# Value products on two column halves of TensorE, normalised from PSUM by VectorE

## The reference, cut to what matters

```python
y = x * rsqrt(mean(x * x, -1) + 1e-6) * rms_w            # x: 2 x 1024 x 512, float32
q, k, v = split(einsum('bsm,cm->bsc', y, w_in))          # 32 query heads in 8 groups, 8 k/v heads, 64 wide
q, k = rope(q), rope(k)                                  # per group: 4 query heads share one k and one v
qk = where(causal, q @ k^T * 64 ** -0.5, -inf)           # 1024 x 1024 per head
attn = softmax(qk)
o = einsum('bghsp,bgxpd->bghsd', attn, v)                # the value products
x = layernorm(x + (x + einsum('bsc,mc->bsm', o, w_out)))
x = layernorm(x + ternary(x) @ (ternary(weight) + rram_variation)^T)
```

## Time and profile before

| | us |
|---|---|
| median of 3 runs | 1427.19 (1426.4 to 1428.69) |
| span of the profiled execution, first to last instruction | 1425.4 |
| first value product starts at | 58.1 |
| TensorE, VectorE, ScalarE, GpSimd busy | 1318.0, 1147.2, 1116.3, 873.7 |
| TensorE's granted clock, mean of the span | 0.982 |

### The profile page before, as it was taken

The page is one execution under the profiler, slowest core; times in us unless marked ns, Lnnn a source line. Parts: engine busy times, 40 slices in busy tenths (PEclk is TensorE's granted clock), DMA queues, the critical chain, the costliest instruction groups (busy, mean ns, idle before and its releaser), DMA issues. The chain is left out here.

```text
span 1425.4 us, 25329 instructions
## 1 busy us (share of the span) xinstructions
PE 1318.0 (92%) x7328; PEld 838.4 (59%) x7328; DVE 1147.2 (80%) x3062; ACT 1116.3 (78%) x2327; POOL 873.7 (61%) x905
## 2 busy tenths in 40 slices
PE   4689999999999999999999999999999999898886
PEld 2456565665656565665656565666656566565554
DVE  4578887878887888878887888878788787887976
ACT  4768878788888888788887878788887888787664
POOL 1266667386645766386646766387646767786565
PEclk9799999999999999999999999999999999999998
DMA  6101111011101211021101211021100211210002
GB/s 199 27 20 38 64 30 31 27 57 45 37 21 45 59 29 31 23 60 44 36 24 26 72 35 31 23 60 43 38 24 23 75 35 37 61 42 27 18 33 85
DMA packets 45163, 61.82 MB, mean 43 GB/s; under 512 B 10464, under 2 KB 27104, under 8 KB 45024
## 3 DMA queue, kind: packets, MB, share of 16 engines
q1 hardware_dynamic: 45024, 60.20, 14.3%
HBM read 34.74 MB, written 4.46 MB: 27 GB/s over the span
## 5 line engine op out<-in xcount | busy, mean ns | idle before, releaser
L1100 DVE SCALAR_TENSOR_TENSOR prob_lo<-t,prob_hi 128x512 f16<-128x512 f32 x576 | 394.7, 686 | 76.0 <-ACT prob_hi L797 72.2
L797 ACT ACTIVATE prob_hi<-t 128x512 f16<-128x512 f32 x576 | 340.2, 591 | 146.1 <-PE t L1221 140.8
L1165 PE MATMUL s<-k_t,q_t 128*128 128x512 f32 (+3 forms) x1536 | 428.2, 383 | 23.8 <-DVE neg_max L1009 8.5
L829 ACT ACTIVATE prob<-prob,neg_max 128x896 f32<-128x896 f32 (+7 forms) x512 | 392.0, 767 | 7.2 <-DVE neg_max L1009 4.3
L1221 PE MATMUL t<-ident,prob 128*128 128x128 f32 x2304 | 350.8, 275 | 6.9 <-ACT prob L829 6.8
L1221 PEld LDWEIGHTS t<-ident,prob 128*128 128x128 f32 x2304 | 290.6, 143 | 109.7 <-ACT prob L829 13.2
L1009 DVE CUSTOM_DVE_ANT_0 prob<-s,mask 128x512 f32<-128x512 f32 (+3 forms) x512 | 289.6, 583 | 53.4 <-PE s L1165 33.3
L1165 PEld LDWEIGHTS s<-k_t,q_t 128*128 128x128 f32 x1536 | 244.9, 193 | 66.4 <-DVE neg_max L1009 19.0
L1136 PE MATMUL ot<-prob_lo,v_sb 128*128 128x512 f16 x576 | 221.0, 384 | 27.1 <-DVE prob_lo L1100 27.0
L1134 PE MATMUL ot<-prob_hi,v_sb 128*128 128x512 f16 x576 | 223.9, 389 | 0.9 <-DVE o_raw L1081 0.9
L770 POOL TENSOR_TENSOR o_lo<-o_raw,o_hi 128x256 f16<-128x256 f32 x128 | 86.2, 674 | 198.7 <-ACT o_hi L907 196.9
(11 more groups left out here) (106 smaller groups left out, 1841.4 us busy)
## 6 DMA issues: line engine op xcount, KB each, us to landing
swapped<-flat SPq DMA_DIRECT2D x320, 64.0 KB, 2.0
spread<-recip_rows SPq DMA_DIRECT2D x128, 128.0 KB
recip_rows<-turned SPq DMA_DIRECT2D x512, 0.5 KB
raw<-L_attn_w_in SPq DMA_DIRECT2D x8, 768.0 KB, 4.2
raw<-L_attn_w_out SPq DMA_DIRECT2D x8, 512.0 KB, 3.6
out<-acc SPq DMA_DIRECT2D x16, 256.0 KB, 2.0
acc<-L_attn_x SPq DMA_DIRECT2D x3, 1024.0 KB, 10.4
acc<-L_attn_x SPq DMA_DIRECT2D x4, 256.0 KB, 4.2
```

What stands on the lines that cost most here:

```text
L797: act.activation(prob_hi[:, u % 2, :], t_ps[u % 2][:, :], ACT.Copy, scale=P_SCALE).then_inc(prob_hi_done, 1)
L829: act.activation(row, row, ACT.Exp, bias=neg_max[:, kk % 4, h:h + 1], scale=-1.0, accum_out=total[:, kk % 4, h:h + 1]).then_inc(ex_done, 1)
L1100: dve.scalar_tensor_tensor(out=prob_lo[:, u % 2, :], in0=t_ps[u % 2][:, :], scalar=P_SCALE, in1=prob_hi[:, u % 2, :], op0=ALU.mult, op1=AL ...
L1165: mm = pe.matmul(s_ps[:, off:off + cols], q_t[:, h, s * P:(s + 1) * P], k_t[:, part, keys:keys + cols], start=(part == 0), stop=(part == 1))
```

## The change

The value products of a unit are made as three pairs: v's low part with `prob_hi`, v's high part with `prob_hi`, v's high part with `prob_lo`; the product low x low is left out. A pair is two matmuls with 64 stationary columns and 256 moving columns: heads 0 and 2 into PSUM partitions 0 to 63, heads 1 and 3 into partitions 64 to 127, all six added in PSUM. For this the transposes put the heads in the order 0, 2, 1, 3. The bank then holds the sum as `o_raw` wants it, in 256 columns. ScalarE's copy and VectorE's two additions ("oe") go; "on" moves from GpSimd to VectorE and multiplies the 128 x 256 of PSUM by `spread` in one operation. TensorE's wait before a bank's next row is now for "on". "on" is put at least 16 steps behind the row's end and before TensorE's need of it, "rs" at most 20 steps behind "rc".

```diff
-        put(spread, ("rs", b, s))
+        put(min(spread, norm + 20), ("rs", b, s))
...
-            put(STEPS * end + lag, (kind, b, s))
+            if kind == "on":
+                lag = max(2 * STEPS, min(lag, STEPS * (units_of(b * NT + s + 1) + 2) - 1))
+            if kind != "oe":
+                put(STEPS * end + lag, (kind, b, s))
...
+def units_of(k):
+
+    return k % NT + 1
...
-                        elif e[0] == "on":                                   # GpSimd
-                            _, b, s = e
-                            kk = b * NT + s
-
-                            wait(pool, o_raw_done, g, 2 * NT, kk + 1)
-                            wait(pool, spread_in[kk % 2], g, 16 * NT, 16 * (kk // 2 + 1))
-                            pool.tensor_tensor(o_raw[:, :, :], o_raw[:, :, :], spread[:, kk % 2, :, :], ALU.mult
-                                               ).then_inc(o_t_done, 1)
...
-                        elif e[0] == "oe":                                   # ScalarE
-                            wait(act, pv_done, g, BODY, b * UNITS + first_unit(s + 1))
-                            wait(act, o_raw_done, g, 2 * NT, k)
-                            act.activation(o_low[:, :], ot_ps[k % 2][DH:P, :], ACT.Copy, scale=1.0 / P_SCALE
-                                           ).then_inc(o_low_done, 1)
...
-                        elif e[0] == "oe":                                   # VectorE
+                        elif e[0] == "on":
                             _, b, s = e
                             kk = b * NT + s
-                            wait(dve, o_low_done, g, 2 * NT, kk + 1)
+
+                            wait(dve, pv_done, g, BODY, b * UNITS + first_unit(s + 1))
+                            wait(dve, spread_in[kk % 2], g, 16 * NT, 16 * (kk // 2 + 1))
                             wait(dve, o_lo_done, g, 2 * NT, kk)
-                            top = ot_ps[kk % 2][0:DH, :].rearrange("p (c a q) -> p a c q", c=2, a=2)
-                            low = o_low[:, :].rearrange("p (c a q) -> p a c q", c=2, a=2)
-                            for a in range(2):
-                                mm = dve.scalar_tensor_tensor(out=o_raw[a * DH:(a + 1) * DH, :, :], in0=top[:, a],
-                                                              scalar=1.0 / P_SCALE, in1=low[:, a], op0=ALU.mult, op1=ALU.add)
-                            mm.then_inc(o_raw_done, 1)
+                            dve.scalar_tensor_tensor(out=o_raw[:, :, :],
+                                                     in0=ot_ps[kk % 2][:, 0:2 * P].rearrange("p (c q) -> p c q", c=2),
+                                                     scalar=1.0 / P_SCALE, in1=spread[:, kk % 2, :, :],
+                                                     op0=ALU.mult, op1=ALU.mult).then_inc(o_t_done, 1)
...
-                        wait(pe, o_raw_done, g, 2 * NT, k - 1)
-                    values_t = v_sb[:, b % 2, j, :]
-                    pe.matmul(ot_ps[k % 2][:, :], values_t, prob_hi[:, u % 2, :], start=(j == 0), stop=False)
+                        wait(pe, o_t_done, g, 2 * NT, k - 1)
+                    v_hi, v_lo = v_sb[:, b % 2, j, 0:DH], v_sb[:, b % 2, j, DH:P]
+
+                    def product(values_t, part, first, last):
+                        for a in range(2):
+                            mm = pe.matmul(ot_ps[k % 2][a * DH:(a + 1) * DH, 0:2 * P], values_t,
+                                           part[:, u % 2, a * 2 * P:(a + 1) * 2 * P], start=first, stop=last)
+                        return mm
+
+                    product(v_lo, prob_hi, j == 0, False)
+                    product(v_hi, prob_hi, False, False)
                     wait(pe, prob_lo_done, g, BODY, u + 1)
-                    pe.matmul(ot_ps[k % 2][:, :], values_t, prob_lo[:, u % 2, :], start=False, stop=(j == s)
-                              ).then_inc(pv_done, 1)
+                    product(v_hi, prob_lo, False, j == s).then_inc(pv_done, 1)
...
-                            mm = pe.transpose(t_ps[u % 2][:, h * P:(h + 1) * P],
+                            at = (h % 2 * 2 + h // 2) * P
+                            mm = pe.transpose(t_ps[u % 2][:, at:at + P],
                                               prob_row(s, h)[:, j * P:(j + 1) * P], ident[:, :])
```

More of the change, by code:

```diff
@@ L334, in seq_block @@
         prob_lo = sb("prob_lo", [P, 2, BANK], F16)
-        o_low = sb("o_low", [DH, BANK])
         o_raw = sb("o_raw", [P, 2, P])
@@ L411, in seq_block @@
         pv_done = sem("pv_done")
-        o_low_done = sem("o_low_done")
-        o_raw_done = sem("o_raw_done")
         o_t_done = sem("o_t_done")
@@ L646, in pool_idle @@
                     wait(pool, o_scale_done, g, 1, 1)
-                elif kind == "on":
-                    wait(pool, o_t_done, g, 2 * NT, what[0] * NT + what[1] + 1)
                 elif kind == "oh":
@@ L664, in one @@
                     for e in plan.ahead[u] + plan.behind[u]:
-                        if (e[0] not in ("ln", "res", "sq", "ro", "hl", "on", "oh", "fl", "x1", "nw", "no")
+                        if (e[0] not in ("ln", "res", "sq", "ro", "hl", "oh", "fl", "x1", "nw", "no")
                                 or plan is first and e[0] in ("ro", "hl")):
@@ L892, in one @@
                                 mm.then_inc(parts_hi, 1)
-                        elif e[0] == "oe":
-                            _, b, s = e
-                            k = b * NT + s
-                            wait(act, pv_done, g, BODY, b * UNITS + first_unit(s + 1))
-                            wait(act, o_raw_done, g, 2 * NT, k)
-                            act.activation(o_low[:, :], ot_ps[k % 2][DH:P, :], ACT.Copy, scale=1.0 / P_SCALE
-                                           ).then_inc(o_low_done, 1)
                         elif e[0] == "oh":
```

## The result

The changed kernel takes **1487.65 us** (median of 4 runs, 1485.67 to 1489.77) against 1427.09 for the kernel before (median of 4 runs): ratio 1.043, 95% interval 1.0411 to 1.0449, so 60.6 us slower. The forecast was 1516, slower, with 1367 to 1600 as range.

A forecast was written before the change was run, and what follows sets the result against it. The prediction took TensorE's issue rate as the bound. The profiled span plus net shape-change cost less absorbed idle time, 1425.4 + 133 - 44 = 1514 us, plus 1.8 us to the runs' median, gave 1516 us; range 1367 to 1600.

The forecast's parts named there:

- step 1: TensorE's value products: three side-by-side pairs take 327 ns per unit instead of 432, a gain of 60 us.
- Rival B: Value products: the two halves do not overlap and switches cost nothing, 1511 to 1555 us; chance 0.10.
- step 2: Two array shape changes per unit on TensorE, 168 ns each; net of the column gain +231 ns per unit, +133 us.
- the turning point: Cost per change of array shape at which the column gain is used up: 105 / 2 = 52 ns.
- Rival A: Changes of array shape on TensorE nearly free: 1367 us; chance 0.38 together with the rival of VectorE's new wait.
- E: Rival: TensorE's column gain and shape switches cancel, nothing measurable changes, 1424 to 1430 us; chance 0.05.
- rival C: TensorE pays tail and exposed loads at both switches, 288 ns each: 1654 us; chance 0.05.
- step 3: TensorE's idle time in the steady middle, partly for prob_lo, absorbs some of the slowdown: -44 us.
- steps 4, 5, 7, 8: ScalarE's copy, VectorE's additions, GpSimd's multiplication, TensorE's wait for o_t_done, the last row's shorter chain: each taken as 0.
- step 6: VectorE's "on" newly waits for the row's last value product and the spread DMA: taken as 0, bounds 0 and +40 us.

The follow-up runs named there:

- one_half_six: Changed kernel, but in the 448 units that do not begin a row all six value products use one column half, heads 1 and 3 omitted there: 1603.8 us.
- full_array_256: Changed kernel, but three full-array products of 256 columns per unit replace the pairs, heads 1 and 3 left out, no change of shape: 1391.2 us.
- before_on_dve: Kernel before, with "on" moved from GpSimd to VectorE behind "oe" and "rs" placed as in the change: 1451.3 us.

## Why the prediction was right, and where it was off

1. **Column work** (step 1, -60 us): right. A pair starts within 3 ns, pairs stand 106 to 109 ns apart, and one_half_six shows what it would cost without overlap. Rival B falls. The sentence of the Trainium skill on column tiles agrees: about 4 ns was stated, 3 ns measured. Today's loads, which I said the pitch does not show, cost 11 ns in the 334 units after scores, so the 432 ns of the kernel before are 443 there.

2. **Changes of shape** (step 2, +133 us): the mechanism was right, the term was too large. Against 168 ns a change, the starts show a wait of 93 ns on the way in and 97 on the way out (206 against 109). My bound, the drawn tail of a product, overstates what must be waited for. The other half of the step, that loads go ahead as they do now, was too low: the weight load of the transposes, which began a whole product early, begins with them, the second pair comes 24 ns late and the second transpose 56. Together it is 270 ns per unit in place of 336, so the step is 576 x (270 - 105) = 95 us, less the 4 us of the 11 ns above, 91 where the sum has 133. This is the term of the sum that was mis-sized. At 135 ns each change costs 2.6 times the 52 ns of the turning point, so rivals A and E fall and the sign holds; rival C, 288 ns a change, falls on the other side. The Trainium skill's rule (TensorEngine Tiling (Array Packing), Key Properties) agrees: a change of mode costs. The rows add that a change between float16 products and float32 transposes on the full array costs nothing (701.31 to 701.52 in the earlier trace rows, a plain pitch).

3. **Idle time that takes it up** (step 3, -44 us): right. The runs give 91 us of TensorE and 14 for the spread wait; 60.6 were measured, so some 44 us were absorbed. That is a remainder, but the starts bear it out. Take each start's distance from the one before, and count as wait what lies above the tenth percentile of its kind (operation, shape and neighbours): over the whole trace these waits sum to 142 us before and 108 after, 35 us less, with the spread wait already in the 108, while the rest grew by 94. The wait for prob_lo that I named fell by 17 us (27.0 in the earlier trace rows to 10.5).

4. **The other engines** (steps 4, 5, 7, 8): their busy times fell as forecast, and with TensorE the slower one it was worth nothing. Where TensorE gains, that cover is thin: full_array_256 got 34 of 60 us, before_on_dve paid 25. Rival A's 1367 was too low for this reason: full_array_256, the nearest run to it, took 1391.

5. **The new wait** (step 6, taken as 0, bound +40): it cost 14 us, within the bound. I had read from the tables that a row or two per pass keep little distance, and then dismissed it with the slower TensorE. The step that failed is that sentence: at row 10 the distance was 7 steps.

So the sum was off by two terms that went against each other: the changes of shape were priced 42 us too high, and the new wait, 14 us, was left out: 1516 - 42 + 14 = 1488. That the forecast came within 28 us is in part luck, since inside step 2 a tail priced too high met loads priced too low. That the time lay in the range says little by itself, since 1367 to 1600 held both signs; what the runs bear out is the sign and its cause.

## What to carry to other kernels

Splitting TensorE's columns saves streaming time only if much half-array work stands together: here a round trip of shapes costs some 270 ns, and a unit's saving of 105 ns pays for it on TensorE only with three units or more at a time. Even then the waits of the regrouped schedule took more than was left. Count the changes of array shape in the instruction order before counting columns. And when a wait moves to a busier engine, look for the one place in the schedule where its distance is shortest, since that place repeats with every pass.

## What the runs showed of the hardware

- A change from 128 x 128 to 128 x 64 products makes the next start 88 to 94 ns later than the plain pitch, a change back 97 to 99, whatever stands on the full-array side (512-column products, float32 transposes, a 128-column dummy). Behind it, the second pair of half-array products comes 24 ns late and the second float32 transpose 56 ns late; the smaller delays look like loads that are no longer covered, which no run tested.
- So a round trip of such products and transposes costs 270 ns, nearly 2.5 products of 256 columns.
- The two column halves take work out of program order against each other: three products for one half followed by three for the other take as long as three alternating pairs (1489.3 against 1487.7 us). The recorded starts on one half stand 10 ns apart there, where one_half_six has 109, so a recorded start on a busy half can be some 100 ns early.
- A product of 256 columns costs 109 ns on the full array and on half of it; a half used alone brings nothing.
